# Reloading x during attention's last turn, five steps of a transfer queue moved by sixteen

## The reference

```python
xn = layernorm(x)
x = x + gatv2(xn, edges) + lambda_mix(xn)     # attention over edges, and a global mixing term
x = x + mixture_of_experts(layernorm(x))      # 8 experts, one per token
```

```python
e = leaky_relu(xl[s] + xr[d]);  score = (e * att).sum per head
alpha = softmax of score over the edges of one destination d
out[d] = sum of alpha * xl[s];  h = elu(out + bias) + xn;  h = layernorm(h) * gamma + beta
```

## Time and profile before

| what | value |
|---|---|
| device time, three runs | 1674.7, 1683.7, 1691.71 us (median 1683.7) |
| span of the profiled execution, first to last instruction | 1339.1 us |
| its own device time | not listed; the median lies 344.6 us above the span |
| busy: PE, DVE, ACT, POOL | 1121.7, 1084.1, 835.9, 820.7 us |
| mean granted PE clock | 0.925 of full speed |
| `attend`, from the first `sum_edges` to the barrier | 103.1 to 1019.0 us |

### The profile page before, as it was taken

One profiled execution on the slowest core, in us unless ns is written; L12 is line 12 of the kernel. 1 busy time (PEld: TensorE's weight loads), 2 busy tenths in 40 slices (PEclk: granted clock), 3 DMA queues, 4 the chain that ended last, 5 costly groups with the idle time before them and its releaser, 6 DMA issues. The chain is left out here.

```text
span 1339.1 us, 24930 instructions
## 1 busy us (share of the span) xinstructions
PE 1121.7 (84%) x5659; PEld 828.3 (62%) x5659; DVE 1084.1 (81%) x2307; ACT 835.9 (62%) x3252; POOL 820.7 (61%) x849
## 2 busy tenths in 40 slices
PE   6959799999879899989988788888867653999994
PEld 4527676767667677767766666676645552565652
DVE  7758899999989989989999899999984982053535
ACT  3421388898868879868888687898853321323230
POOL 6557277777777777777777777777634644022133
PEclk9979899999989999989999899999978665999997
DMA  7576388888878878878787787888712444236320
GB/s 199 152 228 175 100 206 220 217 221 220 212 197 220 219 199 216 217 201 221 217 216 215 192 215 217 218 214 207 215 53 72 129 145 161 88 98 178 100 86 16
DMA packets 167497, 237.47 MB, mean 177 GB/s; under 512 B 40112, under 2 KB 134017, under 8 KB 167406
## 3 DMA queue, kind: packets, MB, share of 16 engines
q1 hardware_dynamic: 123310, 130.22, 34.3%
q0 software_dynamic: 41216, 103.67, 30.5%
q10 hardware_dynamic: 2880, 2.66, 0.6%
HBM read 189.57 MB, written 48.91 MB: 178 GB/s over the span
## 5 line engine op out<-in xcount | busy, mean ns | idle before, releaser
L1508 ACT ACTIVATE e_prod<-gathered_rows,e_prod 128x64 f32<-128x64 f32 x2728 | 670.4, 334 | 5.7
L1079 POOL DMA_INDIRECT gathered_rows<-d_xl,e_idx x576 | 548.8, 953 | 186.3 <-issue 148.7
L1453 PE MATMUL bank<-e_prod,e_selt 128*128 128x260 f32 x1408 | 364.4, 404 | 46.4 <-ACT e_prod L1508 28.9
L1453 PEld LDWEIGHTS bank<-e_prod,e_selt 128*128 128x128 f32 x1408 | 268.5, 198 | 113.4 <-ACT e_prod L1508 50.9
L1399 PE MATMUL bank<-e_xr,e_sel 128*128 128x256 bf16 x2112 | 294.1, 276 | 11.6 <-DVE e_sel L1145 11.6
L1404 PE MATMUL bank<-gathered_rows,ident 128*128 128x256 f32 x704 | 221.3, 397 | 49.1 <-DMA gathered_rows<-d_xl,e_idx 43.3
L1399 PEld LDWEIGHTS bank<-e_xr,e_sel 128*128 128x128 bf16 x2112 | 206.7, 99 | 79.9 <-issue 16.8
L1170 DVE TENSOR_REDUCE e_score<-e_edge 128x16 f32<-128x1024 f32 x176 | 212.3, 1206 | 0.3
L1404 PEld LDWEIGHTS bank<-gathered_rows,ident 128*128 128x128 f32 x704 | 109.1, 196 | 64.2 <-DMA gathered_rows<-d_xl,e_idx 52.5
L1948 POOL DMA_INDIRECT out_dram<-f_out,f_index x32 | 45.4, 1418 | 159.9 <-DVE f_out L2063 155.0
L1153 DVE TENSOR_TENSOR e_edge<-bank,gathered_rows 128x512 f32<-128x512 f32 x176 | 118.7, 675 | 27.4 <-PE bank L1404 27.3
(11 more groups left out here) (315 smaller groups left out, 1094.4 us busy)
## 6 DMA issues: line engine op xcount, KB each, us to landing
e_xr<-d_xr SPq DMA_DIRECT2D x176, 192.0 KB
d_hist<-e_acc SPq DMA_DIRECT2D x176, 130.0 KB
e_drow<-d_rel SPq DMA_DIRECT2D x176, 128.0 KB
w_rows<-in_L_ffn_w_dram SPq DMA_DIRECT2D x16, 1024.0 KB, 7.3
gathered_rows<-d_xl,e_idx POOLq DMA_INDIRECT x576, 4.7
d_in<-lambda_w SPq DMA_DIRECT2D x18, 350.7 KB
e_rows<-d_rows SPq DMA_DIRECT2D x22, 192.5 KB
x_rows<-in_x_dram SPq DMA_DIRECT2D x8, 512.0 KB, 5.0
```

Source lines behind the costliest of these rows:

```text
L1079: pool.indirect_dma_start(xl[:, q.slot * G + g, :], None, m.d_xl, bass.IndirectOffsetOnAxis(ap=column, axis=0)).then_inc(gathered[q.slot], 16)
L1453: last = pe.matmul(ps_agg[b], selt[:, b, g, :], flat(prod[:, b, g, :, :]), start=(g == 0), stop=(g == G - 1))
L1508: last = act.activation(prod[:, b, g, h, 0:HEAD], xl[:, q.slot * G + g, h * HEAD:h * HEAD + HEAD], ACT.Copy, scale=prod[:, b, g, h, HEAD:H ...
```

## The change

The five reloads go from SP's steps 176 to 180 to its steps 160 to 164, the first five of the last turn (QUADS = 176, RING = 16, FOURS = 5). There each stands behind `load(q)` (and, in step 160, `load_rows`) and ahead of `store(q-16)`. `settle` adds one increment of a semaphore that nobody waits for. POOL's additions are not touched.

```diff
                 if b == 0:
                     sp.wait_ge(sl["ctxps"], 1)
+                    settle(sp, m)
                 sp.dma_start(m.x[:, tiles, :], a.x[...]).then_inc(sl["x"], 16)
...
-                if q.known() and QUADS <= q.k < QUADS + FOURS:
-                    reload(q.k - QUADS)
+                if q.known() and QUADS - RING <= q.k < QUADS - RING + FOURS:
+                    reload(q.k - (QUADS - RING))
                 if q.since(STORE_LAG):
                     store(q.ago(STORE_LAG))
```

## The result

In one comparison on one chip the kernel before took 1674.7 us and the changed kernel 1657.27 us (medians of nine runs each). The paired ratio is 0.9943, with a 95% interval of 0.9915 to 0.9972: 0.57% faster, 9.5 us of 1674.7 (4.7 to 14.2). The two medians are 17.4 us apart, 7.9 more than the paired ratio gives; the nine runs of before spread over 27.7 us and those of the change over 10.8, and I go by the ratio.

The account below looks back on a forecast made before the run. POOL's gathers set the attention stage's pace and the DVE, PE and ACT chain closing the last run its end; 9.8 - 2.0 - 0.3 = 7.5 us off 1683.7 gave 1676.2, range 1667 to 1686.

Parts of the forecast that it names:

- the 344.6 us around the span: Time outside the profiled span of 1339.1 us, taken as unchanged, so the difference was applied to the median 1683.7.
- The additions come early: Behind the last quad, POOL's additions start at about 966.0 instead of 977.9, clear of DVE's closing chain: 9.8 us won.
- the chain's 5.8 us: DVE's L1226, L1232 and L1240 in the last run lose their excess beside POOL's additions: 5.8 us won in full.
- the clock: PE's closing groups stay at the higher clock after a pause of 2.4 to 4 us: 3.6 plus 0.4 us won.
- "Nothing" for L1250: Freeing DVE's held-up L1246 and L1250 was said to win nothing, as they stand beside PE's slow group.
- What the additions now meet: Early additions collide with DVE's L1208, L1202 and L1220 in quads 174 and 175: 2.0 us lost, between 1.6 and 3.0.
- The first rival: The collision only moves: the fifth addition precedes L1202, PE's slow groups stay, 2.8 us won, 1680.9; chance 0.10.
- The transfers: Reloads on top of loads in steps 160 to 164 pile up 4.0 us, against 3.7 of DVE pauses: 0.3 us lost.
- The second rival: Reloads delay gathered rows and stall the stage: two stalls leave 0.9 us won, chance 0.15; three or more slower, 0.06.
- POOL's last gather: Sign in the attention stage: still at 964; if later, gathers were held back and the prediction is wrong.
- The barrier: Sign at the end of the attention stage: the barrier near 1011.5, where the earlier profile had 1018.97.

Follow-up runs that it names:

- e0: The kernel before, with no edit, profiled on a chip of the later batches; device time 1341.15 us, span 1339.4 us.
- e1: Kernel before, reloads at their old place, POOL's additions made to wait until DVE's raise_more of the last run; ratio to before 0.9947.
- e2: Changed kernel with early reloads, POOL's additions made to wait for DVE's scan_back of the last run; ratio to before 0.9990.
- e6: Changed kernel with POOL's five additions left out, so x lacks its constant row; ratio to before 0.9915.
- e4: The changed kernel, with no edit, on a chip where before takes about 1341 us; ratio to before 0.9958.
- e11: The changed kernel once more, with no edit, in another batch; ratio to before 0.9961.
- e7: Changed kernel with the reloads ten steps later, in SP's steps 170 to 174; ratio to before 0.9949.
- e8: Changed kernel with POOL's additions in twenty pieces of one tile in place of five of four tiles; ratio to before 0.9963.
- e9: Kernel before, reloads at their old place, POOL's additions in twenty pieces of one tile; ratio to before 0.9965.
- e3: Changed kernel with early reloads, POOL's additions made to wait until DVE's raise_more of the last run; ratio to before 0.9955.
- e5: Changed kernel with all five reloads in step 160 in place of one in each of steps 160 to 164; ratio to before 0.9986.

## Why the prediction was right in its mechanism and wrong in its time

**The time.** The step that failed is the base: "I take the 344.6 us around the span as unchanged and apply the difference to the median". Hardly anything lay around the span: e0 had 1.75 us there, and the profiled execution of after 1.8 (1662.86 of device time, 1661.1 of span). The 344.6 us lay inside executions of another kind. The forecast started from 1683.7, the median of three runs that spread over 17 us; nine runs of before in the comparison gave 1674.7, 9.0 us less. That alone takes the forecast from 1676.2 to 1667.2, the lower end of the range. The text did say that such a median may be off by some 5 us; it was off by 9. Of the 9.9 us from there to 1657.27 the gain explains 2.0 (9.5 and not 7.5); the other 7.9 are the difference between the two medians and the paired ratio, and stay unexplained.

**The additions come early.** Right, and it is the cause (e1, e2). 9.8 us were expected; e6 shows 8.7 in the tail and 10.3 to 11.4 in the time. Inside it the chain's 5.8 us went in full, in e4, e11 and e6. That leaves 2.9 us of e6 (8.7 - 5.8) for the clock, which was charged with 4.0, and not all of that is the clock's. "Nothing" for L1250 was wrong. ACT's timeline in the profile of before:

```profile
990.45 0.20 ACT L1497 ACTIVATE e_rr<-e_drop 1x4 f32<-1x4 f32 x1 [13.42 <-DVE e_drop L1250]
990.57 0.21 ACT L1504 ACTIVATE e_prod<-e_diff 128x16 f32<-128x16 f32 x1
990.81 2.02 ACT L1508 ACTIVATE e_prod<-gathered_rows,e_prod 128x64 f32<-128x64 f32 x8
```

L1250, held up to 990.42, held ACT, whose products for PE's second group were ready at 992.83, and that group started at 993.08 after a wait of 1.30 us (the row names a selection table that had ended just as late, at 992.85; by the order in e6 this group uses the one before, which was ready at 986.9). In e6 ACT had gone on at 981.90 and the wait was 0.22 us; in e2, where L1252 was held the same way, it was 1.30 again. So some 1.1 us come from L1246 and L1250, and about 1.8 from the clock: groups of 2.80 and 3.49 us where before had 3.80 twice, and what follows them.

**What the additions now meet.** Right in place, half in size: this is the term that was mis-sized. 2.0 us were taken, between bounds of 1.6 and 3.0. In e4 DVE lost 1.0 + 2.2 = 3.2 us and in e11 1.6 + 2.2, or 3.7: the fifth addition went ahead of L1203, and both are above the upper bound. Choosing by the row of 3.20 us, where DVE had kept the pair, was the wrong choice; order between the two engines is not fixed (in e7 L1209 was held for 1.5 us and L1203 for none). What had no place in the sum is what follows on PE. From the last sum_edges to L1226 it took 12.26 us in e4 (970.59 to 982.85) and 7.43 in e6 (971.07 to 978.50): 4.8 us, 3.2 of them DVE's and 1.6 the slow group ahead of the transposes. With what comes behind, e4's tail is 6.1 us longer than e6's (45.9 - 39.8), and 4.3 by the times. The first rival, the collision that only moves, was thus half true: it named this mechanism, and gave it 0.10. Its price, 2.8 us won, is lower than the 5.2 to 5.6 measured. By the tails it is nearer: e4's is 2.6 us shorter than that of the profile of before, e11's 4.0. Where the rest of the measured gain lies these single executions do not show. The port rule of the Trainium skill, page "SBUF — State Buffer", section "Who interferes with whom", held for all that was seen (for a copy or a tensor_scalar, which has one input, the page says that it can contend in a mode that uses both ports): each instruction held up had two inputs in SBUF or was a copy or a tensor_scalar on SBUF (L1146 1.64 us, L1203 2.84), and the one with a PSUM input, L1236 in e2, took 0.38 between two that were held.

**The clock.** "A pause of 2.4 to 4 us should leave it at the higher clock" failed. Pauses of 3.35 and 3.50 us gave groups of 3.81 and 3.80 us (e8, e9), one of 2.52 gave 3.68 (e4), but 2.54 in e11, and 2.29 or 2.30 gave 1.99 in e3 and after, 2.43 in e7, 2.67 in e1 and 2.80 in e6. Two rows of one pause each could not carry the rule. The length of the pause alone does not decide. Right ahead of it stood pauses of 2.10 and 0.65 us in e4 and of 1.58 and 0.58 in e3; whether that is what decides is not shown.

**The transfers.** 0.3 us were charged, and nothing or a small gain came. A share of 1.00 was reached, as forecast (above 0.9), but nothing piled up: DVE was busy for 24.93 of 25 us. The prediction summed busy shares per step as if they were work that can't be pressed together. The lower end that it named is what happened. The last sum_edges starts 5.9 and 5.4 us behind the last gather in e4 and e11, against 6.2 or 6.3 in the three profiles of before; but it is 8.4 us in e6, with the same reloads, so the place of the reloads is not shown to be the reason. The Trainium skill, page "SBUF — State Buffer", section "Summary: rules for kernel authors", gives some 358 GB/s, by which nothing was to pile up, and the trace agrees: the mean of 303 GB/s in e4 lies below it. As a bound it did not hold in windows of 5 us: e4 moved 364 GB/s and e11 370 (893 to 898).

**The second rival** did not come, in e4, e11 or e7. e5 shows that a stall exists, and that in it DVE waited for loads behind SP's held queue, not for the gathered rows that the rival spoke of; the waits of 0.30 and 0.78 us for `e_xr` in e11 and e6 are of the same kind. **POOL's last gather** kept its time (964.67, 965.18). **The barrier** came at 1016.49 and 1015.06, not at 1011.5; it did in e6, at 1010.89, with no additions.

**The sum on this kind of chip:** 7.5 us forecast, 5.2 to 5.6 measured, with upper ends of 7.2 (e4) and 7.6; short by the collisions and by PE's clock behind them. In the first comparison 9.5 us. A reason can be read from the profile after, where POOL is 18.6 us ahead and its additions meet neither L1209 nor L1203; that is argued from one profile and was not tried, as no experiment ran in such a condition.

## What to carry to other kernels

Moving a transfer is worth what it lets start: look for the work behind its wait (here POOL's additions), and list what of the neighbouring engine with two SBUF inputs stands beside that work at the old place and at the new one, then charge the full length of one instruction for each meeting, with PE's clock behind it. Follow each instruction that is held to every engine that waits for it: L1250 looked hidden behind PE and held ACT. Compare the profiled execution's own span with the timed runs before using the one for the other: if they are hundreds of microseconds apart, the profile is of another kind of execution, and only differences or ratios carry over. Transfers that are spread by a step each filled the DMA engines here with little harm, while the same bytes in one step held the issuing queue and the small loads behind them.

## What was unexpected of the hardware

- The same program took about 1341 us on three chips and 1664 to 1692 us in the first comparison. There, in the profile of the change, PE, DVE and ACT stood still together in many places (0.00 busy from 606 to 608) while POOL and transfers went on. What holds them stays open.
- SP's issues took 8.80 us for five transfers when all were issued in one step, against 0.40 us for one (e4).
- The DMA share read 1.06 and 1.07 in e5, at 341 and 357 GB/s, 1.07 in e4 at 364 and 1.08 in e11 at 370, so a share of 1.00 is not yet the most that they move.
- PE's clock after a pause of 2.29 us: lower for a part of the group in e6 (2.80 us, granted clock 0.69), higher in e3 and after (1.99 us; 1.00 in e3).
